# Row landings awaited on VectorE itself, and SyncE's tables read four pairs at a time, in a two-layer graph kernel

## What is computed

```
# layer 0: 4 heads of 32
kj    = k[src] + e                       # e: projected edge attributes
alpha = einsum('ehc,ehc->eh', q[dst], kj) / sqrt(32)
expa  = exp(alpha - segment_max(alpha, dst)[dst])
alpha = expa / segment_sum(expa, dst)[dst]
out   = segment_sum((v[src] + e) * alpha, dst)
# then a gate, a projection, x1 = layernorm(x + ...)
# layer 1: one head of 256, scores from x1
scores  = sum(q[dst] * k[src], -1) / 16 + edge_weight * we + be
attn    = softmax of scores over the edges of one dst
message = segment_sum(v[src] * attn, dst)
# then layernorm, feed-forward, layernorm, and a last residual and layernorm
```

## Time and profile before

| what | value |
|---|---|
| time, median of 3 runs | 4909.48 us |
| lowest and highest run | 4899.42 and 4911.46 us |
| span of the profiled execution | 4909.6 us |
| VectorE busy | 3800.3 us, 77% |
| TensorE busy | 3789.0 us, 77% |
| GpSimd busy | 3298.3 us, 67% |
| ScalarE busy | 2933.3 us, 60% |

### The profile page before, as it was taken

The page is one execution under the profiler, slowest core; times in us unless marked ns, Lnnn a source line. Parts: engine busy times, 40 slices in busy tenths (PEclk is TensorE's granted clock), DMA queues, the critical chain, the costliest instruction groups (busy, mean ns, idle before and its releaser), DMA issues.

```text
span 4909.6 us, 110612 instructions
## 1 busy us (share of the span) xinstructions
PE 3789.0 (77%) x25147; PEld 3208.0 (65%) x25147; DVE 3800.3 (77%) x12902; ACT 2933.3 (60%) x7020; POOL 3298.3 (67%) x3637
## 2 busy tenths in 40 slices
PE   7677777777777777776768888888888887887898
PEld 4566666666666666664546666666666676675787
DVE  4688888888888888886747777767677677776788
ACT  1567776777677677763336666665666665665332
POOL 1777777777777777762367777777777777775455
PEclk9798899899899999898978998989898889899999
DMA  6788888887888888873468888888888888886222
GB/s 199 207 217 214 215 216 216 214 217 213 216 216 215 217 215 212 213 189 94 124 182 227 231 237 233 230 231 234 230 239 232 225 229 237 233 237 188 75 80 66
DMA packets 746042, 996.39 MB, mean 203 GB/s; under 512 B 189632, under 2 KB 503168, under 8 KB 745392
## 3 DMA queue, kind: packets, MB, share of 16 engines
q1 hardware_dynamic: 454336, 481.61, 36.5%
q0 software_dynamic: 150224, 410.39, 31.8%
q10 hardware_dynamic: 140832, 97.33, 6.4%
HBM read 862.96 MB, written 125.90 MB: 201 GB/s over the span
## 4 chain that ended last, share of the span: by engine, by line
PE 26%; DVE 19%; issue 14%; DMA 13%; DVEq 11%; POOL 9%; ACT 3%; ACTq 2%; POOLq 1%; SPq 1%
PE ps L1336 25%; DMA acc_d<-acc 9%; POOL rows L621 8%; DVE score L980 4%; DVE rows L968 3%; DVEq L1192 2%; DVEq L1190 2%; DVE acc L1133 2%; DVEq L1172 2%; DMA dst_row<-in_dst_row 2%; DMA rows<-kv_d,src_all 1%; ACT place L705 1%; DVE msg L1108 1%; ACTq L755 1%; DVE prod L975 1%
## 5 line engine op out<-in xcount | busy, mean ns | idle before, releaser
L621 POOL DMA_INDIRECT rows<-kv_d,src_all x1564 | 1527.6, 977 | 640.1 <-issue 458.5
L621 POOL DMA_INDIRECT rows<-x_d,src_all x1564 | 1484.2, 949 | 540.7 <-issue 440.7
L1336 PE MATMUL ps<-place 128*128 128x256 bf16 (+2 forms) x10560 | 1334.0, 277 | 138.2 <-ACT place L705 134.2
L1336 PEld LDWEIGHTS ps<-place 128*128 128x128 bf16 (+1 forms) x10560 | 1129.7, 140 | 321.9 <-issue 110.7
L701 ACT ACTIVATE place<-dst_row,node_tab 128x512 f32<-128x512 int32 (+1 forms) x880 | 615.4, 710 | 623.4 <-DMA acc_d<-acc 409.7
L1336 PE MATMUL ps<-rows,oh 128*128 x3520 | 882.2, 400 | 59.1 <-DVE oh L1113 33.2
L992 DVE SCALAR_TENSOR_TENSOR prod<-rows,ps 128x256 f32<-128x256 f32 x1760 | 637.3, 418 | 296.0 <-PE ps L1336 188.1
L711 ACT ACTIVATE oh<-iota_row,rel 128x128 f32<-128x128 f32 x2640 | 828.6, 386 | 16.3 <-DMA acc_d<-acc 7.9
L1336 PEld LDWEIGHTS ps<-rows,oh 128*128 128x128 f32 x3520 | 668.6, 198 | 153.3 <-issue 63.1
L1336 PE MATMUL ps<-msg,oh 128*128 128x132 f32 x3520 | 496.1, 287 | 213.5 <-DVE msg L1108 116.1
L705 ACT ACTIVATE place<-place,ones 128x512 f32<-128x512 f32 (+1 forms) x880 | 622.9, 720 | 54.2 <-issue 1.7
(11 more groups left out here) (216 smaller groups left out, 4164.1 us busy)
## 6 DMA issues: line engine op xcount, KB each, us to landing
dst_row<-in_dst_row SPq DMA_DIRECT2D x880, 256.0 KB
place<-q_d SPq DMA_DIRECT2D x440, 192.8 KB
acc_d<-acc ACTq DMA_DIRECT2D x440, 128.5 KB
ea<-in_eaT SPq DMA_DIRECT2D x440, 128.0 KB
acc_d<-acc ACTq DMA_DIRECT2D x440, 66.0 KB
place<-q_d SPq DMA_DIRECT2D x440, 64.0 KB
rows<-kv_d,src_all POOLq DMA_INDIRECT x1564
rows<-x_d,src_all POOLq DMA_INDIRECT x1564
```

What stands on the lines that cost most here:

```text
L621: pool.indirect_dma_start(out=L.rows[:, t % SLOTS, j, 0:D], out_offset=None, in_=L.table, in_offset=bass.IndirectOffsetOnAxis(ap=src_all[: ...
L1336: return pe.matmul(out_, lhsT=lhsT, rhs=rhs, start=first, stop=last)
```

## The change

SyncE no longer tells of landings: tell_landed() and the semaphore "landed" go. VectorE waits itself on the two gather semaphores, just where it waited for "landed", with counts that it reads into registers: load_landings() reads 16 counts (8 pairs, two each) for the next chunk at the seventh pair of a chunk, and at the start of a layer for the first. These counts have no range check at run time; each is used as "count & LANDED_MASK", which leaves the values as they are. SyncE reads pair_tab, now three numbers wide, for four pairs at a time, in load_pair() and in load_idx(). What is computed is the same, and so are all the DMAs of data.

```
@@ -47,6 +47,7 @@
 ONE_HOTS = ((), (), (2, 3), (4,), (5, 6), (7,), (), ())
 SLOTS = 2 * CH
 NO_NODE = 1 << 20
+LANDED_MASK = (1 << 14) - 1
 BY_DVE = 2
 U = 4
 EPS = 1e-5
@@ -131,7 +132,7 @@
         base_tab = sb("base_tab", [P, NPAIR])
         node_tab = sb("node_tab", [P, NPAIR])
         keep_tab = sb("keep_tab", [P, NPAIR])
-        pair_tab = sb("pair_tab", [1, NPAIR, 4], I32)
+        pair_tab = sb("pair_tab", [1, NPAIR, 3], I32)
         land_tab = sb("land_tab", [1, NPAIR, 2], I32)
         slot_tab = sb("slot_tab", [1, NPAIR], I32)
         start_tab = sb("start_tab", [1, SG * P], I32)
@@ -261,6 +262,12 @@
             return zip(range(CH * c, CH * c + CH),
                        load_row(engine, slot_tab[0:1, CH * c:CH * c + CH], 0, SLOTS - 1, "the table holds t & 15"))
 
+        def load_landings(engine, c):
+
+            both = load_row(engine, land_tab[0:1, CH * c:CH * c + CH, :].rearrange("o g n -> o (g n)"), 64, 64 * NS,
+                            "the table holds 64 times one to half of the steps")
+            return zip(range(CH * c, CH * c + CH), [(even & LANDED_MASK, odd & LANDED_MASK) for even, odd in zip(both[0::2], both[1::2])])
+
         def window(ap, w):
             return ap[bass.ds(w, 1)].rearrange("o p c -> (o p) c")
 
@@ -297,7 +304,7 @@
 
         def edge_sems(n):
             names = ("oht", "e", "q", "score", "masked", "turned", "pens", "ends", "arranged", "carries", "spreadback",
-                     "landed", "full", "fullT", "below", "prob", "shrink_in", "shrink", "so_in", "so", "msg", "msgp", "agg",
+                     "full", "fullT", "below", "prob", "shrink_in", "shrink", "so_in", "so", "msg", "msgp", "agg",
                      "acc", "first", "added")
             s = {x: sem(f"l{n}_{x}") for x in names if n == 0 or x not in ("e", "added")}
             for x in ("gathered", "stored"):
@@ -426,11 +433,16 @@
                 def free_idx(c):
                     wait(s["masked"], c - 1)
 
+                idx_steps = {}
+
                 def load_idx(c, par, steps):
 
                     for st in steps:
+                        if st % 4 == 0:
+                            g = CH * c + st
+                            idx_steps.update(zip(range(g, g + 4), load_row(ENGINE.SP, pair_tab[0:1, g:g + 4, :].rearrange("o g n -> o (g n)"))[0::3]))
                         wait(s_idx[st], 16 * c)
-                        t = sp.value_load(pair_tab[0:1, CH * c + st, 0:1])
+                        t = idx_steps.pop(CH * c + st)
                         sp.dma_start(idx[par][:, st, :], a["idx"][bass.ds(t, 1)].rearrange("o p c -> (o p) c"))\
                           .then_inc(s_idx[st], 16)
 
@@ -445,22 +457,22 @@
                     wait(s_idx[0], L.idx_before + 16 * c)
                     sp.dma_start(idx[par][:, :, :].rearrange("p s j -> p (s j)"), window(idx_d, c)).then_inc(s_idx[0], 16)
 
-                landing = {}
+                pair_rows = {}
 
                 def load_pair(g, par, st):
 
                     place = st % PLACES
-                    t, w, te = load_row(ENGINE.SP, pair_tab[0:1, g, 0:3])
-                    if g % 2 == 0:
-                        both = load_row(ENGINE.SP, land_tab[0:1, g:g + 2, :].rearrange("o g n -> o (g n)"), 64, 64 * NS)
-                        landing[g], landing[g + 1] = both[0:2], both[2:4]
-                    b = place
+                    if g % 4 == 0:
+                        four = load_row(ENGINE.SP, pair_tab[0:1, g:g + 4, :].rearrange("o g n -> o (g n)"))
+                        pair_rows.update((g + m, four[3 * m:3 * m + 3]) for m in range(4))
+                    row = pair_rows.pop(g)
+                    t, w, b = row[0], row[1], place
                     sp.dma_start(dst_row[place][:, :], a["dst_row"][bass.ds(t, 1), :].partition_broadcast(P))\
                       .then_inc(s["ld_row"][b], 16)
                     sp.dma_start(L.qw[place], window(L.q_d, w))\
                       .then_inc(s["ld_q"][b], 16)
                     if L is L0:
-                        sp.dma_start(ea[place][0:DR, :], a["eaT"][:, bass.ds(te * SUPER, SUPER)])\
+                        sp.dma_start(ea[place][0:DR, :], a["eaT"][:, bass.ds(row[2] * SUPER, SUPER)])\
                           .then_inc(s["ld_ea"][b], 16)
 
                 def load_ahead(c, par, st):
@@ -470,13 +482,6 @@
                         wait(s["first"], c + 1)
                     wait(s["q"], g - 1)
                     load_pair(g + 2, (par + (st + 2) // CH) % 2, (st + 2) % CH)
-
-                def tell_landed(g):
-
-                    even, odd = landing.pop(g)
-                    sp.wait_ge(s["gathered"][0], even)
-                    sp.wait_ge(s["gathered"][1], odd)
-                    sp.sem_inc(s["landed"], 1)
 
                 def emit(c, par, scores, sums):
                     if not scores:
@@ -492,8 +497,6 @@
                     for st in range(CH):
                         if more(c, st + 2):
                             load_ahead(c, par, st)
-                        tell_landed(CH * c + st)
-
                         if st == (1 if L is L0 else 2) and not last:
                             free_idx(c + 1)
                             if L is L0:
@@ -953,6 +956,14 @@
                 s, H, R = L.s, L.H, L.R
                 slot = {}
 
+                landings = {}
+
+                def landed(g):
+
+                    even, odd = landings.pop(g)
+                    v.wait_ge(s["gathered"][0], even)
+                    v.wait_ge(s["gathered"][1], odd)
+
                 def first_node(c, par):
 
                     v.wait_ge(s["ld_row"][0], loads_done(L, c, 0))
@@ -963,7 +974,7 @@
 
                     b = st % 2
                     kv = held(kv_rows, slot[CH * c + st]).rearrange("p j (m n) -> p j m n", m=2)
-                    v.wait_ge(s["landed"], CH * c + st + 1)
+                    landed(CH * c + st)
                     v.wait_ge(s["e"], CH * c + st + 1)
                     v.tensor_tensor(kv, kv, e_ps(b).rearrange("p (j n) -> p j n", j=JT).unsqueeze(2)
                                     .to_broadcast([P, JT, 2, DM]), ALU.add).then_inc(s["added"], 1)
@@ -986,7 +997,7 @@
 
                     g, b = CH * c + st, st % 2
                     x1 = held(x1_rows, slot.pop(g))
-                    v.wait_ge(s["landed"], g + 1)
+                    landed(g)
                     v.wait_ge(s["q"], g + 1)
                     for j in range(JT):
                         i = v.scalar_tensor_tensor(
@@ -1138,6 +1149,7 @@
                     if scores:
                         if not sums:
                             slot.update(load_slots(ENGINE.DVE, c))
+                            landings.update(load_landings(ENGINE.DVE, c))
                         first_node(c, par)
                         if L is L0:
                             add_edges(c, par, 0)
@@ -1181,6 +1193,8 @@
                             weigh(past, pp, r)
                         if st == 5 and more(c + 1, 0):
                             slot.update(load_slots(ENGINE.DVE, c + 1))
+                        if st == 6 and more(c + 1, 0):
+                            landings.update(load_landings(ENGINE.DVE, c + 1))
                         if st >= 2:
                             next(masking, None)
                         if sums and st == 2:
```

## The result

The changed kernel takes 4959.53 us (median of 4 runs, 4955.14 to 4968.24) where the kernel before takes 4910.47: a ratio of 1.0112, with a 95% interval of 1.0096 to 1.0127. It is 1.1% slower; 4972 us was forecast, inside the forecast's own range.

A forecast was written before the change was run, and what follows sets the result against it. VectorE's own stream, sequencer included, was taken to bound the first layer, with GpSimd's gathers and VectorE close together in the second. 4909.5 + 79 (first layer) - 12 (second) - 5 (starts) gave about 4972 us, own range 4940 to 5005.

The forecast's parts named there:

- The masks: First layer, VectorE's waits before the edge addition: two bare masks cost 0.18 us a pair, 79 us in all.
- all "issue": Expected sign at the edge addition: idle time of 0.4 to 0.5 us, which the profile would put down wholly to issue.
- The counts' read: VectorE, seventh pair of a chunk: reading sixteen registers takes 1.2 us, hidden under 1.74 us of work, so costs nothing.
- Starts: Start of both layers: first loads no longer stand behind index reads and checks, -5 us (0 to -12).
- The second layer: Second edge layer: masks' cost and earlier loads' gain together give -12 us.
- +18 for the masks: Second layer: masks cost 36 us at pairs not waiting for TensorE, about half taken back by the chunk's next wait.
- -30 for the loads: Second layer: SyncE's earlier loads let a quarter of ScalarE's 131.6 us wait for node rows reach GpSimd's pace.
- charges nothing for earlier loads: Second layer: earlier loads meet gathers on DMA engines 85% busy; same bytes, so no charge, up to 20 us as bound.
- it relieves nothing: First layer: SyncE's cheaper reads don't help VectorE, whose waits for others there are a few us.
- The masks cost nothing: Rival: masks fold in or are computed at the read; about 4900 us; chance 0.17, shared with the relay-hidden rival.
- the read sticks out: Rival: the counts' read outlasts VectorE's covering work; 5030 us, chance 0.05; without any cover 5103 us, chance 0.03.
- SyncE's freedom pays: Rival: earlier loads bring the second layer to the gathers' floor, -68 us; 4850 us, or 4884 at half; chance 0.20.

The follow-up runs named there:

- Experiment 9: Changed kernel with first-layer counts masked twice at VectorE's wait and SyncE also waiting for both counts in the second layer: 5051.59 us against 4937.52 before, ratio 1.0239.
- experiment 5: Changed kernel with each pair's masks worked out two pairs ahead instead of at the wait behind the drain: 4941.0 us against 4904.59 before, ratio 1.0075.
- 12: Relay in first layer, direct waits in second, SyncE holding first-layer third-pair loads until an earlier second-pair store lands: 4906.64 us against 4920.62 before, ratio 0.9967.
- experiment 10: Changed kernel with SyncE's relay and VectorE's constant wait back in the first layer, direct waits in the second: 4943.17 us against 4919.21 before, ratio 1.0038.

## Why the prediction was right, and where it was not

**The masks.** Right in place, kind and size. They stand at the wait lines, two a pair, bare behind the drain; 79 us was forecast as 440 x 0.18, the addition's idle time rose by 72.7 us (0.165 a pair) and the layer by 65. Experiment 9 adds two more and gets 56 us in 54 chunks; experiment 5 moves them and takes 56 us from the idle time. One sign was wrong: the idle time was to be all "issue", and the profile calls 38.2 of the 189.2 us so, because the register waits now stand among the masks.

**The counts' read.** Right: 1.10 us for sixteen registers, 1.2 forecast, hidden under 1.74. By the Trainium skill, "Runtime: NRT & Kernel Launch", section "Instruction fetch mechanics", with about 200 ns a register, an estimate for sixteen is 3.2 us; the run shows a third of that. The passage is about loads over an uncached path that the runtime's own instructions make, and this table lies in on-chip memory. So the run shows that the figure doesn't carry over to such a table, not that it is wrong for its own loads.

**Twelve registers in SyncE.** 0.9 us forecast, 0.748 measured.

**Starts.** -5 forecast, -4.3 measured. In experiment 5 it is -1.9, in 12 -0.3, so the agreement may well be luck.

**The second layer.** -12 us forecast, -16 measured in one pair of traces. The mechanism (late node rows and late queries go away) is shown, by their disappearance and by their partial return in 9. The gain in time isn't, and neither is its division into +18 for the masks and -30 for the loads, which no run separates: with direct waits, the five traces have chunks of 36.69, 36.77, 36.88, 37.15 (experiment 10) and 37.19 us (12), before 36.98. The chip and the execution move it by more than the change does, so that -16 came close to -12 is luck. VectorE waits for rows in place of queries, as the earlier trace rows would have it: GpSimd stands close to its own pace.

**The step that failed, without harm to the total**, is the one that charges nothing for earlier loads, because "the bytes are the same". I set it in the second layer and against gathers. The loads do collide, in the first layer, with the accumulator's stores, for 28 us where VectorE isn't slowed. The changed kernel doesn't pay it: the store takes 4.30 us, and the masks bring VectorE to it only after 5.1. So the two costs don't add: 65 us with the masks, 28 us without (10), about 0 with the loads held. It also shows that "it relieves nothing", said of SyncE's cheap reads in the first layer, was too kind to them.

**The rivals.** "The masks cost nothing" and "the read sticks out" did not occur. "SyncE's freedom pays" said it decides below 0.17 us a pair on VectorE. At no cost on VectorE at all (10) the kernel was still 0.4% slower. So that point was wrong. With the loads held as well (12) it was 0.3% faster, by a path that the traces don't show.

## What to carry to other kernels

On an engine that sets the pace, a register instruction behind a drain is idle time, nearly one for one; work out register values while an operation runs, or let an idle engine turn the register wait into a wait on a constant. When a queue gets cheaper, list what its transfers will now run beside: here a store with a short deadline, and a wait of one line put the old spacing back on purpose. If moving a cost away gives back less than its idle time, look for the wait that has become the next one, before blaming what is left of the old.

## What had not been expected of the hardware

- The same program on the same kind of chip can run at 6730 to 6860 us in place of 4910, at a mean granted clock of 0.79 in place of 0.91, with TensorE issuing single multiplications 1.4 to 2.2 us apart. Two chips showed both at different times. What withholds the instructions was not tested.
- A store of 66 KB issued 0.7 us after the first of three loads of 256, 64 and 128 KB landed 1.3 us later (median over the layer, experiment 10) than one issued 3.5 us ahead of them (before), while the 16 DMA engines were busy 0.81 of the time on average with the collision and 0.82 (before) or 0.83 (experiment 12) without it. An average hides a collision of this kind.
- The extra register instructions took 0.07 us each in idle time where the first two took 0.083, for durations of 0.040. In the changed kernel's trace, ahead of the addition at 1252.30 us, they start 0.087 us apart.
